# Keys, values and weight quantisation of the second layer moved into the expert stage of a two-layer gated cross-attention kernel

## The chip, the cores and the metric

The kernel runs on one core of a Trainium2 chip. The metric is the device time of one execution in microseconds (us), as the median of several runs. Engines: PE is TensorE, ACT is ScalarE, DVE is VectorE, POOL is GpSimd, SP is SyncE, which here only issues DMAs; SPq is SP's queue of DMA issues.

## What is computed

Two layers over 64 sequences of 128 tokens and 256 channels, in float32. Each layer adds a gated cross-attention and a gated feed-forward part to the residual:

```
x = x + tanh(g_xattn[0]) * attention0(layernorm(x), ctx)      # 16 heads of 16 channels, keys of one sequence: 128
x = x + tanh(g_ffn[0])   * experts(layernorm(x))              # router, 64 experts, top 8, at most 256 tokens each, + a shared one
x = x + tanh(g_xattn[1]) * attention1(layernorm(x), ctx, mask)
x = x + tanh(g_ffn[1])   * quantised_ffn(layernorm(x))        # int8-like activations and weights, 704 wide
```

Keys and values of both layers come from `ctx`, which no earlier step changes: `k = ctx @ wk.T + bk`, `v = ctx @ wv.T + bv`. A token's routing weight for an expert is `2.5 * sigmoid(logit) / (sum over its 8 chosen)`. The last part quantises its three weight matrices by row: `clip(round(w / scale)) * scale` with `scale = max|w| / 127`.

## The kernel before, in words

The work is in five phases, separated by `phase_end`, where all engines wait for each other.

1. Loads and constants.
2. First layer's attention, with router and shared expert. A loop over slots: in slot s each engine does its steps for several sequences at once, each at a fixed lag (`stage(lag)` is sequence s - lag). The residual lies in `res` (64 rows of 256 floats per partition). The part after the attention goes to memory: `store` puts residual plus shared expert into `accumulator`, `store_row` puts the normalised token with one float of routing share (`pay`, ROW = 257 floats) into `token_rows`. In the last slots, and after them, DVE quantises the weights of the last part (`weights_dve`), PE transposes them (`weights_pe`), ACT copies them (`weights_act`), SP stores them (`ffn_weights_out`). Before the phase ends, SP issues the second layer's weights (`attention_weights`) and the first experts' (`first_expert_weights`).
3. Experts (`experts_pe`, `_act`, `_dve`, `_pool`, `_sp`). One slot for each of 64 experts. DVE and PE work out which tokens an expert has (`slot_steps`, `tokens`), two slots ahead POOL gathers their rows from `token_rows` by two indirect DMAs (`gather`), PE transposes them (`rows_t`), multiplies by the two upper matrices (`up`) and, with 1-column products, by the router's column (the logits again), and then by the lower matrix (`down`). DVE multiplies by the routing weight (`outputs`), and POOL adds the rows to `accumulator` by two indirect DMAs (`add`). After the last expert PE and ACT make keys and values of sequences 0 to 2 (`first_keys_values_pe`, `_act`).
4. Second layer's attention: 64 slots and a few for the ends. For sequence b the steps are: SP loads the context `cx` and the two accumulators' rows `ax` (`load`, three slots ahead); DVE adds the two (`first_sum`, L852, two slots ahead) and takes statistics; ACT normalises; PE projects q, k and v (`project_qk` L434, `project_v` L449); ACT copies them out (`copy_qk` L621 and L624, `copy_v` L634); PE writes the mask and the scores into the four banks of `tiles` (L336, L352), DVE takes the maximum of all four (L810), PE writes mask and transposed scores into the same banks (L336, L369), ACT takes the exponent (L601), PE multiplies by the values (L399), transposes (L480), DVE divides (`head_norm`, L918), PE transposes back (`tokens_to_heads`, L490) and multiplies by the output matrix (L469).
5. The quantised part in two passes.

Each engine runs its own instructions strictly in the order written, and waits on counting semaphores. In phase 4 the order on DVE in a slot is: maximum, `first_sum`, `first_stats`, `head_sums`, `head_norm`, `token_maximum`, `residual`, and so on. On PE it is: mask and scores, the projections, mask and transposed scores, `heads_to_tokens`, `output`, `tokens_to_heads`, `transposes`, `maxima_t`, `values`. On SP it is only:

```
wait(sp, sm("v_done"), b - 3)
wait(sp, sm("qk_done"), b - 3)
load_context(sp, b, r)
...
wait(sp, sm("sum_done"), b - 1)
for n_ in range(2):
    sp.dma_start(ax[p][:, n_, :], acc[n_][bass.ds(b * P, P), :]).then_inc(sem(f"ax_in{p}"), 16)
```

`v_done` and `qk_done` count PE's projections. The first wait is for the projections of sequence b - 4.

Of the kernel before, what the change touches and what calls it, by code (L numbers as in the profile page):

```python
# [5 lines left out]
def flamingo_gated_two_layers(nc: bass.Bass, a, out: bass.AP):  # L6
# [25 lines left out]
    ROW = D + 1  # L32
    SHAREC = D
# [16 lines left out]
    KV_FIRST = 3  # L50
# [11 lines left out]
    hidden_away = nc.dram_tensor("hidden_away", [len(AWAY), P, IC * CT], f32).ap()  # L62
    ffn_int = nc.dram_tensor("ffn_int", [3, P, KC * IP], bf16).ap()

    ctx = ExitStack()
    with ctx:
# [86 lines left out]
        xr = ring("xr", 4, [P, HALVES, ROW])  # L153
        xrt = ring("xrt", 2, [P, KC, CAP])
        sg = ring("sg", 2, [P, CAP])
        he = ring("he", 2, [P, CAP])
        ye = ring("ye", 4, [P, HALVES, D])
        wcol = ring("wcol", 4, [P, HALVES])
        tid = ring("tid", 8, [P, HALVES], i32)
        ehs = ring("ehs", 2, [P, CAP])  # L160
        ren = ring("ren", 2, [P, HALVES])
# [52 lines left out]
        wraw = [qkp[:, 3 * n:3 * n + 3, :].rearrange("p a (c d) -> p (a c) d", d=D) for n in range(2)]  # L214
        wdraw = cxax[:, 0:6, :].rearrange("p a d -> p (a d)")[:, 0:KC * I].rearrange("p (k i) -> p k i", k=KC)
        wq_b = pt[1][:, 2:4, :].rearrange("p a d -> p (a d)").bitcast(bf16)[:, 0:KC * IP]
        ws = [w.rearrange("p a d -> p (a d)").bitcast(bf16)[:, 0:KC * IP] for w in (pt[0][:, 2:4, :], ovs[:, :, :], qkp[:, 0:2, :])]
# [78 lines left out]
        MADE_WEIGHTS = (8 if IREST else 6) * 2 + 11  # L296
# [26 lines left out]
        TILES_IN_0 = 8 * NB  # L323
# [3 lines left out]
        def attention_pe(pe, L):  # L327
            def sm(name):
                return f"{name}_{L}"

# [8 lines left out]
            def scores(m):  # L339
# [4 lines left out]
                wait(pe, sm("exp_done"), b - 1)  # L344
# [9 lines left out]
                last.then_inc(sem(sm("s_done")), 1)  # L354

            def scores_t(k):
# [4 lines left out]
                pe.wait_ge(sem(sm("max_done")), ahead(b, 2))  # L361
                if L == 1:
                    masks(1)
                pe.wait_ge(sem(sm("qm_done")), b + 1)
# [6 lines left out]
                last.then_inc(sem(sm("st_done")), 1)  # L371

            def maxima_t(m):

                if m is None:
                    return
                b, _ = m
                pe.wait_ge(sem(sm("max_done")), b + 1)
# [6 lines left out]
                nc.tensor.transpose(bk[:, 0:P], mt[:, :], ident[:, :]).then_inc(sem(sm("mt_done")), 1)  # L385

            def values(k):
# [5 lines left out]
                pe.wait_ge(sem(sm("exp_done")), b + 1)  # L393
                pe.wait_ge(sem(sm("v_out")), b + 1)
                wait(pe, sm("at_out"), b)
# [5 lines left out]
                last.then_inc(sem(sm("pv_done")), 1)  # L401

            def transposes(f):
# [8 lines left out]
                else:  # L412
                    wait(pe, sm("v_out"), b)
# [4 lines left out]
            def project_qk(f):  # L418
# [5 lines left out]
                pe.wait_ge(sem(f"tile_in{r}"), (2 - L) * (4 * (b - r) + 16) + L * TILES_IN_0)  # L424
# [5 lines left out]
                for j in range(KC):  # L430
                    for n, w in enumerate((w_q, w_k)[:1 if L == 1 and b < KV_FIRST else 2]):
# [4 lines left out]
                last.then_inc(sem(sm("qk_done")), 1)  # L436

            def project_v(f):
                if f is None or (L == 1 and f[0] < KV_FIRST):
                    return  # L440
                b, r = f
                pe.wait_ge(sem(f"tile_in{r}"), (2 - L) * (4 * (b - r) + 16) + L * TILES_IN_0)
                if L == 0:
                    wait(pe, sm("silu_done"), b - 4)
                    wait(pe, sm("qm_done"), b - 1)
                else:
                    pe.wait_ge(sem(sm("xt_out")), b + 1)
# [3 lines left out]
                last.then_inc(sem(sm("v_done")), 1)  # L451

            def output(k):
# [4 lines left out]
                pe.wait_ge(sem(sm("at_out")), b + 1)  # L458
                if L == 0:
                    wait(pe, sm("x2t_out"), b)  # L460
                else:
                    pe.wait_ge(sem(sm("qm_done")), ahead(b, 3))
# [10 lines left out]
            def heads_to_tokens(k):  # L473
# [4 lines left out]
                pe.wait_ge(sem(sm("ov_out")), b + 1)  # L478
                for g in range(NG):
                    last = nc.tensor.transpose(bank[7][:, g * P:(g + 1) * P], ov[r % 2][:, g, :], ident[:, :])  # L480
                last.then_inc(sem(sm("ot_done")), 1)

            def tokens_to_heads(k):
# [4 lines left out]
                pe.wait_ge(sem(sm("on_done")), b + 1)  # L488
                for c in range(KC):
                    last = nc.tensor.transpose(bank[7][:, c * P:(c + 1) * P], on[r % 2][:, c * P:(c + 1) * P], ident[:, :])  # L490
                last.then_inc(sem(sm("at_done")), 1)
# [11 lines left out]
            def moe_up(k):  # L503
# [7 lines left out]
                pe.wait_ge(sem(sm("qm_done")), ahead(b, 4))  # L511
# [46 lines left out]
            def body(stage):  # L558
# [17 lines left out]
                else:  # L576
                    project_qk(f)
                    project_v(f)
# [11 lines left out]
        def attention_act(act, L):  # L590
            def sm(name):
                return f"{name}_{L}"

            def exponent(k):
# [4 lines left out]
                act.wait_ge(sem(sm("st_done")), b + 1)  # L599
                wait(act, sm("pv_done"), b - 1)  # L600
                nc.scalar.activation(pt[r % 2][:, :, :], tiles[:, :, :], ACT.Exp).then_inc(sem(sm("exp_done")), 1)  # L601

            def copy_xt(f):
# [4 lines left out]
                wait(act, sm("qk_done"), b - 1)  # L608
# [3 lines left out]
            def copy_qk(f):  # L612
# [4 lines left out]
                act.wait_ge(sem(sm("qk_done")), b + 1)  # L617
                wait(act, sm("st_done"), b - 3)
                wait(act, sm("qm_done"), b - 1)
                for j in range(KC):  # L620
                    last = nc.scalar.activation(qt[p][:, j, :], bank[5][:, j * P:(j + 1) * P], ACT.Identity, bias=qb[:, j:j + 1])  # L621
                    if L == 0 or b >= KV_FIRST:
                        for e in range(2):
                            last = nc.scalar.activation(kp[r][:, e, j, :], bank[5][:, (KC + j) * P:(KC + j + 1) * P],  # L624
                                                        ACT.Identity, bias=kb[:, e, j:j + 1], scale=keep[:, e:e + 1])
                    last.then_inc(sem(sm("qk_out")), 1)

            def copy_v(f):
                if f is None or (L == 1 and f[0] < KV_FIRST):
                    return  # L630
                b, r = f
                act.wait_ge(sem(sm("v_done")), b + 1)
# [1452 lines left out]
```

## Time and profile before

| | |
|---|---|
| median of 3 runs | 2064.66 us (2063.12 to 2065.77) |
| profiled execution | 2069.3 us, of which the span is 2067.5 us |
| busy share of the span | PE 89%, DVE 68%, ACT 54%, POOL 27% |
| mean granted TensorE clock | 0.945 |
| phase 3, experts | 809.1 to 1246.4 us |
| phase 4, second attention, steady part | 1281 to 1837 us |
| chain that ended last | PE 66%, DVE 14%, issue 8%, POOL 5%, DMA 4%, ACT 2% |

Times in rows are microseconds from the start of the span unless marked ns. A timeline row is start, duration, engine, line, operation, output and inputs with their shapes and count, and in brackets the idle time of the engine before it with what ended it. A busy share over the whole span averages phases with different limits, so each phase is read alone.

### The profile page before, as it was taken

How to read it: one execution, taken by the hardware profiler on the slowest of the kernel's cores; microseconds unless marked ns; L12 is line 12 of the kernel's file. 1: busy time of each engine (PE TensorE's matmuls, PEld its weight loads, DVE VectorE, ACT ScalarE, POOL GpSimd, SP SyncE). 2: the span in 40 equal slices, each digit the busy share in tenths (PEclk: the TensorE clock that was granted, in tenths of full speed). 3: DMA queues.
4: the chain of work that ended last, by engine and by line, in shares of the span. 5: the costliest groups of instructions: out<-in, count | busy, mean ns of one | idle time of the engine just before them, and what ended most of it. 6: DMA issues, size and time to landing. Idle time of an engine off the chain costs nothing.

```text
span 2067.5 us, 55165 instructions
## 1 busy us (share of the span) xinstructions
PE 1832.9 (89%) x20966; PEld 1463.2 (71%) x20976; DVE 1402.3 (68%) x4715; ACT 1119.8 (54%) x2347; POOL 562.2 (27%) x551
## 2 busy tenths in 40 slices
PE   6999999999999994888778876999999999978855
PEld 4888888888888873666666664777777777753334
DVE  4778878787878776444444435666666666658988
ACT  3666666666666651111111124666666666658875
POOL 1000000000000001788888871111111111111147
PEclk9999999999999996888888888999999999999989
DMA  3122222222222215666666652111111111102355
GB/s 96 45 60 61 61 64 60 71 61 64 61 63 61 58 43 182 139 140 141 142 141 143 133 98 64 48 41 48 45 43 48 41 48 41 40 25 111 134 214 193
DMA packets 158646, 174.30 MB, mean 84 GB/s; under 512 B 22512, under 2 KB 142704, under 8 KB 156208
## 3 DMA queue, kind: packets, MB, share of 16 engines
q1 hardware_dynamic: 133568, 136.34, 21.9%
q0 software_dynamic: 24816, 34.42, 9.9%
q8 instruction: 170, 2.79, 0.6%
q14 instruction: 92, 0.75, 0.1%
HBM read 104.72 MB, written 65.98 MB: 83 GB/s over the span
## 4 chain that ended last, share of the span: by engine, by line
PE 66%; DVE 14%; issue 8%; POOL 5%; DMA 4%; ACT 2%; POOLq 0%; SPq 0%; DVEq 0%; ACTq 0%
PE bank L434 12%; PE tiles L369 7%; PE tiles L352 7%; PE bank L399 6%; PE bank L517 6%; PE bank L449 5%; PE bank L480 4%; PE bank L469 3%; PE bank L540 3%; PE tiles L1252 3%; DVE hmax L1660 2%; POOL accumulator L1457 2%; PE tiles L336 2%; POOL xr L1442 2%; DMA xr<-token_rows,tid 2%
## 5 line engine op out<-in xcount | busy, mean ns | idle before, releaser
L1920 POOL TENSOR_TENSOR rstd<-var,minus_half 128x2 f32<-128x2 f32 x138 | 96.1, 696 | 1142.9 <-DVE var L887 1142.7
L810 DVE TENSOR_REDUCE mt<-tiles 128x16 f32<-128x2048 f32 x128 | 293.5, 2293 | 113.6 <-PE tiles L352 113.6
L601 ACT ACTIVATE pt<-tiles 128x2048 f32<-128x2048 f32 x128 | 240.8, 1881 | 13.1 <-PE tiles L369 8.5
L1457 POOL DMA_INDIRECT accumulator<-ye,tid x128 | 205.0, 1601 | 42.8 <-issue 31.7
L624 ACT ACTIVATE qkp<-bank,kb,keep 128x128 f32<-128x128 f32 x500 | 205.2, 475 | 0.0
L1405 DVE TENSOR_SCALAR ye<-bank,wcol 128x256 f32<-128x256 f32 x128 | 56.0, 479 | 216.3 <-PE bank L1270 175.1
L434 PE MATMUL bank<-xt,w_q 128*128 128x128 f32 x1024 | 165.1, 285 | 0.9 <-ACT xt L609 0.9
L621 ACT ACTIVATE qkp<-bank,qb 128x128 f32<-128x128 f32 x256 | 96.0, 376 | 123.9 <-PE bank L434 123.7
L1442 POOL DMA_INDIRECT xr<-token_rows,tid x128 | 137.3, 1072 | 81.1 <-DVE within L1370 44.5
L434 PE MATMUL bank<-cxax,w_k 128*128 128x128 f32 x1000 | 154.3, 277 | 0.0
L434 PEld LDWEIGHTS bank<-xt,w_q 128*128 128x128 f32 x1024 | 136.8, 195 | 22.6 <-issue 20.9
L369 PE MATMUL tiles<-qm,qkp 32*128 32x128 f32 x4096 | 150.2, 283 | 1.4 <-DVE mt L810 1.4
L352 PE MATMUL tiles<-qkp 32*128 32x256 f32 x2048 | 148.1, 402 | 3.2 <-ACT qkp L624 3.2
L1321 ACT COPY xrt<-tiles 128x512 f32<-128x512 f32 x64 | 37.5, 586 | 206.6 <-PE tiles L1234 173.2
L369 PEld LDWEIGHTS tiles<-qm,qkp 32*128 32x128 f32 x4096 | 125.8, 186 | 27.2 <-issue 24.3
L399 PE MATMUL bank<-pt,vx 128*32 128x128 f32 x4096 | 138.4, 276 | 2.3 <-ACT pt L601 1.5
L434 PEld LDWEIGHTS bank<-cxax,w_k 128*128 128x128 f32 x1000 | 133.5, 194 | 0.0
L469 PE MATMUL bank<-w_o,at 128*128 128x256 f32 x512 | 131.8, 380 | 0.5 <-ACT at L676 0.5
L667 ACT COPY ovs<-bank 128x512 f32<-128x512 f32 x128 | 75.1, 587 | 102.2 <-PE bank L399 102.2
L449 PE MATMUL bank<-w_v,cxax 128*128 128x256 f32 x500 | 130.2, 383 | 0.0
L1234 PE MATMUL tiles<-ident,xr 128*128 128x128 f32 x256 | 53.0, 342 | 78.9 <-DMA xr<-token_rows,tid 78.9
L352 PEld LDWEIGHTS tiles<-qkp 32*128 32x128 f32 x2048 | 92.7, 185 | 34.9 <-issue 26.9
(255 smaller groups left out, 4079.3 us busy)
## 6 DMA issues: line engine op xcount, KB each, us to landing
cxax<-in_ctx SPq DMA_DIRECT2D x128, 128.0 KB, 2.6
cxax<-accumulator SPq DMA_DIRECT2D x128, 128.0 KB, 2.2
hidden_away<-h_ring SPq DMA_DIRECT2D x8, 1536.0 KB, 5.1
pt<-in_expert_up SPq DMA_DIRECT2D x36, 256.0 KB, 4.6
token_rows<-pay SPq DMA_DIRECT2D x64, 128.5 KB, 2.7
res<-in_x SPq DMA_DIRECT2D x64, 128.0 KB, 2.7
accumulator<-xa SPq DMA_DIRECT2D x64, 128.0 KB, 1.7
accumulator<-zt SPq DMA_DIRECT2D x64, 128.0 KB, 1.8
```

Source lines behind the costliest of these rows:

```text
L352: last = nc.tensor.matmul(both, qt[r % 2][rows, j, :], kp[r][rows, :, j, :], start=(L == 0), stop=True, skip_group_check=(L == 1))
L369: last = nc.tensor.matmul(tiles[:, i, n * P:(n + 1) * P], kp[r][rows, e, j, :], qm[rows, e, j, :], start=(L == 0), stop=True, skip_group_c ...
L399: last = nc.tensor.matmul(bank[7][32 * h:32 * h + 32, g * P:(g + 1) * P], vx[r][:, GH * g + h, :], pt[p][:, i, n * P:(n + 1) * P], start=T ...
L434: last = nc.tensor.matmul(o_, w[:, c, j * P:(j + 1) * P], (cx[r] if n else xt[p])[:, c, :], start=(c == 0), stop=(c == KC - 1))
L449: last = nc.tensor.matmul(bank[4][:, 0:D], cx[r][:, c, :], w_v[:, c, :], start=(c == 0), stop=(c == KC - 1))
L469: last = nc.tensor.matmul(bank[6][:, 0:D], at[r % 2][:, c, :], w_o[:, c, :], start=(L == 1 and c == 0), stop=(c == KC - 1))
L517: last = nc.tensor.matmul(bank[4][:, n * FS + j * P:n * FS + (j + 1) * P], w[:, c, j * P:(j + 1) * P], x2t[p][:, c, :], start=(c == 0), st ...
L601: nc.scalar.activation(pt[r % 2][:, :, :], tiles[:, :, :], ACT.Exp).then_inc(sem(sm("exp_done")), 1)
L624: last = nc.scalar.activation(kp[r][:, e, j, :], bank[5][:, (KC + j) * P:(KC + j + 1) * P], ACT.Identity, bias=kb[:, e, j:j + 1], scale=ke ...
L810: nc.vector.tensor_reduce(mt[:, :].rearrange("p (i n c) -> p i n c", i=RT, n=2 * KC)[:, :, :, 0], tiles[:, :, :].rearrange("p i (n k) -> p ...
L1442: nc.gpsimd.indirect_dma_start(out=xr[r][:, h, :], out_offset=None, in_=rows[:, :], in_offset=bass.IndirectOffsetOnAxis(ap=tid[n % 8][:, h ...
L1457: nc.gpsimd.indirect_dma_start(out=acc[p][:, :], out_offset=bass.IndirectOffsetOnAxis(ap=tid[b % 8][:, h:h + 1], axis=0), in_=ye[r][:, h, ...
```

## The change

- A row of `token_rows` takes the token's 64 routing weights (`pay`, ROW = 320 floats). The router products, their tanh (`route_tanh`) and `wcol` in the experts' phase go; `outputs` multiplies by a column of the gathered row. The gathered rows have 5 buffers, not 4.
- In each expert's slot PE makes keys or values of two sequences (`keys_or_values`: 4 products of 256 columns, even slots keys, odd slots values), ACT copies the bank out (`copy_pair`), SP stores it to `keys_values` (`keep_pair`, 256 KB) and loads the context of a later pair. The rows 8 to 55 of `res`, free in that phase, are the room.
- In phase 4 PE projects q alone. SP loads a sequence's keys and values (2 DMAs into `kvt`, two buffers) where it loaded the context, and ACT copies them from there. `first_keys_values_pe` and `_act` go.
- The quantisation of the weights leaves the end of phase 2: DVE takes one step of it in a slot of the experts, PE, ACT and SP in the slots of `WEIGHTS_AT` and `WEIGHTS_OUT_AT`. Its loads are issued when `xa_done_0` reaches 56.
- Semaphores of both attention phases count on over both layers (`first + b`), which changes no order.

```diff
-    ROW = D + 1
-    SHAREC = D
+    ROW = D + E
+    GATEC = D
+    ROWS_IN = 5
...
+        cxp = [room(44 + 2 * k, 2).rearrange("p (c e t) -> p c e t", c=KC, e=2) for k in range(4)]
+        kvs = [room(52 + 2 * k, 2) for k in range(2)]
+        ROOM_FROM, ROOM_TO = 8, 56
+        kvt = [cxax[:, 2 * k:2 * k + 2, :].rearrange("p a d -> p (a d)") for k in range(2)]
...
-                for n, w in enumerate((w_q, w_k)[:1 if L == 1 and b < KV_FIRST else 2]):
+                for n, w in enumerate((w_q, w_k)[:2 - L]):
...
                 else:
                     project_qk(f)
-                    project_v(f)
                     scores_t(k)
...
+                if L == 1:
+                    act.wait_ge(sem(f"kv_in{p}"), 16 * (b - p) + 32)
...
+                    k = bank[5][:, (KC + j) * P:(KC + j + 1) * P] if L == 0 else kvt[p][:, j * P:(j + 1) * P]
+                    for e in range(2):
+                        last = nc.scalar.activation(kp[r][:, e, j, :], k, ACT.Identity, bias=kb[:, e, j:j + 1], scale=keep[:, e:e + 1])
...
-                st.mark(V.tensor_tensor(pay[r][:, SHAREC:SHAREC + 1], wsum[:, 0:1], tg_route[:, 0:1], ALU.mult))
+                st.mark(V.tensor_scalar(pay[r][:, GATEC:GATEC + E], wun[:, :], wsum[:, 0:1], tg_route[:, 0:1], ALU.mult, ALU.mult))
...
-                if L == 0 or b >= KV_FIRST:
-                    wait(sp, sm("v_done"), b - 3)
-                    wait(sp, sm("qk_done"), b - 3)
+                if L == 0:
+                    wait(sp, "v_done", first + b - 3)
+                    wait(sp, "qk_done", first + b - 3)
                     load_context(sp, b, r)
...
                 else:
+                    wait(sp, sm("qk_out"), 2 * (b - 1))
+                    wait(sp, sm("v_out"), b - 1)
+                    sp.dma_start(kvt[p][:, 0:D].rearrange("p (c t) -> p c t", c=KC),
+                                 keys_values[b - p].rearrange("p (c e t) -> p c e t", c=KC, e=2)[:, :, p, :]).then_inc(sem(f"kv_in{p}"), 16)
+                    sp.dma_start(kvt[p][:, D:2 * D], keys_values[b - p + 1][:, p * D:(p + 1) * D]).then_inc(sem(f"kv_in{p}"), 16)
                     wait(sp, sm("sum_done"), b - 1)
                     for n_ in range(2):
                         sp.dma_start(ax[p][:, n_, :], acc[n_][bass.ds(b * P, P), :]).then_inc(sem(f"ax_in{p}"), 16)
...
+            def keys_or_values(e):
+                if e is None:
+                    return
+                n, _ = e
+                j = n // 2
...
+                pe.wait_ge(sem(f"pair_in{j % 4}"), 8 * (j - j % 4) + 32)
+                wait(pe, "kv_out", n)
+                for k in range(2):
+                    for c in range(KC):
...
+                        last = nc.tensor.matmul(bank[5][:, k * D:(k + 1) * D], weights_, moving, start=(c == 0), stop=(c == KC - 1))
+                last.then_inc(sem("kv_done"), 1)
...
-                for h in range(HALVES):
-                    for c in range(KC):
-                        last = nc.tensor.matmul(bank[7][:, h:h + 1], xrt[p][:, c, h * P:(h + 1) * P], w_gate[:, c, expert_of(b):expert_of(b) + 1],
-                                                start=(c == 0), stop=(c == KC - 1))
-                last.then_inc(sem("e_logit_done"), 1)
...
             def body(stage):
                 slot_steps(stage(-MAP_AHEAD))
                 rows_t(stage(0))
+                keys_or_values(stage(0))
                 up(stage(1))
                 down(stage(2))
...
-        def ffn_weights_out(sp):
-            for n in range(3):
-                sp.wait_ge(sem("w_t_out"), n + 1)
-                sp.dma_start(ffn_int[n], ws[n]).then_inc(sem("ffn_int_out"), 16)
...
+        WEIGHTS_AT = {8: 0, 9: 0, 13: 1, 14: 1, 20: 2, 21: 2, 23: 3}
+        WEIGHTS_OUT_AT = {11: 0, 16: 1, 23: 2}
...
-            attention_dve(dve, 0, ffn_weights)
-            for _ in ffn_weights:
-                pass
+            attention_dve(dve, 0)
```

In phase 4, SP's issues and the waits ahead of them (`cxax` is the tile that holds `cx`, `ax` and, in the change, `kvt`). Before, one sequence is three rows:

```order
L1090 DMA cxax<-in_ctx 128x2x128 [waits qk_done_1,v_done_1]
L1112 DMA cxax<-accumulator 128x256 [waits sum_done_1]
L1112 DMA cxax<-accumulator 128x256
L1090 DMA cxax<-in_ctx 128x2x128 [waits qk_done_1,v_done_1]
L1112 DMA cxax<-accumulator 128x256 [waits sum_done_1]
L1112 DMA cxax<-accumulator 128x256
```

In the changed kernel it is four:

```order
L1122 DMA cxax<-keys_values 128x2x128 [waits v_out_1,qk_out_1]
L1124 DMA cxax<-keys_values 128x256
L1127 DMA cxax<-accumulator 128x256 [waits sum_done_1]
L1127 DMA cxax<-accumulator 128x256
L1122 DMA cxax<-keys_values 128x2x128 [waits v_out_1,qk_out_1]
L1124 DMA cxax<-keys_values 128x256
L1127 DMA cxax<-accumulator 128x256 [waits sum_done_1]
L1127 DMA cxax<-accumulator 128x256
```

The accumulators' rows, which stood behind a wait for PE's projections of sequence b - 4, now stand behind a wait for ACT's copies of sequence b - 2 (`v_out_1`, `qk_out_1`).

On DVE, one slot of phase 4 in the changed kernel (`res<-cxax` is `first_sum` of sequence s + 2, `on` is `head_norm` of sequence s - 3); this order is that of before:

```order
L825 TENSOR_REDUCE mt<-tiles 128x16 [waits mt_done,s_done]
L867 TENSOR_TENSOR res<-cxax 128x256 [waits ax_in0]
L877 BN_STATS st<-res 128x6 [waits sum_done_1]
L924 RECIPROCAL rden<-bank 128x16 [waits ot_done]
L933 TENSOR_TENSOR on<-bank,rden 128x256 [waits at_done,rden_done]
```

Nothing moved here; `head_norm` and all that follows it stand behind the wait for `ax_in`.

## Rows read from the trace of the kernel before

**Rows 1.** Stretches: length, busy PE, PEld, DVE, ACT, POOL, granted clock, DMA share, GB/s.

```profile
809.10:1246.40 437.30, 344.57 (x1705) 281.83 (x1705) 191.65 (x873) 78.36 (x207) 342.24 (x256) 0.83 0.65 132
...
1281.00:1837.00 556.00, 546.57 (x8694) 412.29 (x8692) 372.05 (x834) 377.49 (x777) 84.08 (x118) 1.00 0.15 44
```

**Rows 2.** Timeline of PE in one slot of the second attention.

```profile
1547.87 0.43 PE L336 MATMUL tiles<-mask_bias,identb 32*32 32x512 bf16 x16
...
1549.31 0.71 PE L434 MATMUL bank<-xt,w_q 128*128 128x128 f32 x4
...
1551.20 1.03 PE L449 MATMUL bank<-w_v,cxax 128*128 128x256 f32 x4
1552.15 0.43 PE L336 MATMUL tiles<-mask_bias,identb 32*32 32x512 bf16 x16
...
1555.09 0.44 PE L490 MATMUL bank<-ident,on 128*128 128x128 f32 x2
...
1557.21 0.43 PE L336 MATMUL tiles<-mask_bias,identb 32*32 32x512 bf16 x16
```

**Rows 3.** Timeline of DVE, ACT and SP's queue in the same slot.

```profile
1549.45 2.29 DVE L810 TENSOR_REDUCE mt<-tiles 128x16 f32<-128x2048 f32 x1 [1.04 <-PE tiles L352]
...
1551.40 0.37 ACT L621 ACTIVATE qkp<-bank,qb 128x128 f32<-128x128 f32 x1 [1.82 <-PE bank L434]
1551.65 0.41 DVE L852 TENSOR_TENSOR res<-cxax 128x256 f32<-128x256 f32 x1
...
1552.26 0.38 SPq L1090 DMA_DIRECT2D cxax<-in_ctx  x1
...
1552.68 0.94 SPq L1112 DMA_DIRECT2D cxax<-accumulator  x2
1553.29 0.40 ACT L634 COPY vx<-bank 128x256 f32<-128x256 f32 x1
...
1554.32 0.26 DVE L909 RECIPROCAL rden<-bank 128x16 f32<-128x16 f32 x1 [1.79 <-PE bank L480]
1554.61 0.42 DVE L918 TENSOR_TENSOR on<-bank,rden 128x256 f32<-128x256 f32 x1
```

**Rows 4.** DMA issues: output<-input, count, size, median us from issue to landing.

```profile
cxax<-in_ctx SPq DMA_DIRECT2D x128, 128.0 KB, 2.6
cxax<-accumulator SPq DMA_DIRECT2D x128, 128.0 KB, 2.2
```

**Rows 5.** Timeline of DVE: first and last of the 64 maxima of the second attention.

```profile
1258.27 2.29 DVE L810 TENSOR_REDUCE mt<-tiles 128x16 f32<-128x2048 f32 x1 [1.86 <-PE tiles L352]
...
1836.98 2.29 DVE L810 TENSOR_REDUCE mt<-tiles 128x16 f32<-128x2048 f32 x1 [1.12 <-PE tiles L352]
```

**Rows 6.** Experts: PE's timeline around a wait, and the stretch behind it.

```profile
1109.84 0.66 PE L1234 MATMUL tiles<-ident,xr 128*128 128x128 f32 x4 [2.62 <-DMA xr<-token_rows,tid]
...
1113.14 1.71 PE L1258 MATMUL bank<-w_gate,xrt 128*128 128x1 f32 x8
...
1121.27 0.95 PE L1258 MATMUL bank<-w_gate,xrt 128*128 128x1 f32 x8
...
1110.90:1121.10 10.20, 10.20 (x33) 8.04 (x32) 2.87 (x13) 1.36 (x4) 8.06 (x8) 0.50 0.64 119
```

**Rows 7.** Groups of instructions: POOL's two indirect DMAs of the experts.

```profile
L1457 POOL DMA_INDIRECT accumulator<-ye,tid x128 | 205.0, 1601 | 42.8 <-issue 31.7
...
L1442 POOL DMA_INDIRECT xr<-token_rows,tid x128 | 137.3, 1072 | 81.1 <-DVE within L1370 44.5
```

**Rows 8.** End of phase 2: SP's last expert weights, quantisation steps, PE's next phase.

```profile
802.14 0.43 SPq L1181 DMA_DIRECT2D xt<-in_L_ffn_w  x1
...
L761 DVE TENSOR_REDUCE s_gu<-qkp 128x6 f32<-128x1536 f32 x2 | 3.5, 1748 | 0.2 <-DVE pt L775 0.2
...
L771 DVE TENSOR_SCALAR qkp<-qkp 128x1536 f32<-128x1536 f32 x2 | 1.9, 959 | 0.1
...
809.11 0.22 PE L1209 MATMUL bank<-table,halves_tri 128*128 128x32 bf16 x1 [1.17 <-SPq L257]
```

More of the change, by code:

```diff
@@ L343, in scores @@
                 b, r = m
-                wait(pe, sm("exp_done"), b - 1)
+                wait(pe, "exp_done", first + b - 1)
                 if L == 1:
@@ L435, in project_qk @@
                                                     start=(c == 0), stop=(c == KC - 1))
-                last.then_inc(sem(sm("qk_done")), 1)
+                last.then_inc(sem("qk_done"), 1)
             def project_v(f):
-                if f is None or (L == 1 and f[0] < KV_FIRST):
+                if f is None:
                     return
                 b, r = f
[L442 to L447, printed above, removed]
+                pe.wait_ge(sem(f"tile_in{r}"), 8 * (b - r) + 32)
+                wait(pe, sm("silu_done"), b - 4)
+                wait(pe, "qm_done", first + b - 1)
                 for c in range(KC):
@@ L794, in weights_dve @@
-            st.then(V.tensor_copy(at[0][:, :, :], s_d[:, :].unsqueeze(2).broadcast_to([P, KC, P])))
+            st.mark(V.reciprocal(sig[:, :], sig[:, :]))
+            st.mark(V.tensor_copy(at[0][:, :, :], s_d[:, :].unsqueeze(2).broadcast_to([P, KC, P])))
+            yield
+            for _ in range(5):
+                yield
             dve.wait_ge(sem("sd_t"), 1)
-            st.then(V.tensor_copy(sd_row[:, :], bank[1][:, 0:D]))
+            st.mark(V.tensor_copy(sd_row[:, :], bank[1][:, 0:D]))
@@ L1045, in body @@
                     routing(1)
-                    if v is not None and v[0] == NB - 1:
-                        next(ahead_of_time)
                     routing(1)
@@ L1082, in body @@
                     gate_scales()
-                if L == 0 and v is not None:
-                    for _ in range({NB - 3: 1, NB - 2: 1, NB - 1: 3}.get(v[0], 0)):
-                        next(ahead_of_time)
             attention_slots(body, FIRST[L])
@@ L1329, in gate_tanh, with copy_pair @@
                 nc.scalar.activation(sg[r % 2][:, :], bank[2 + r % 2][:, 0:CAP], ACT.Tanh, scale=0.5).then_inc(sem("e_sg_done"), 1)
[L1331 removed]
+            def copy_pair(e):
                 if e is None:
                     return
[L1334 to L1337 removed]
+                n, r = e
+                p = r % 2
+                act.wait_ge(sem("kv_done"), n + 1)
+                wait(act, f"kv_kept{p}", 8 * (n - p))
+                nc.scalar.copy(kvs[p], bank[5][:, :]).then_inc(sem("kv_out"), 1)
             def body(stage):
                 copy_t(stage(0))
+                copy_pair(stage(0))
                 gate_tanh(stage(1))
[L1342 removed]
+                if stage(0) is not None and stage(0)[0] in WEIGHTS_AT:
+                    next(weights, None)
+            weights = weights_act(act)
             expert_slots(body)
@@ L1425, in body @@
                 hidden(stage(1))
+                if stage(0) is not None and stage(0)[0] > 2 and stage(0)[0] != E // 4 and stage(0)[0] != E // 4 + 4:
+                    next(weights, None)
                 next_layer(stage(0))
+            weights = weights_dve(dve)
             begin()
```

314 lines of the change are left out of this document (152 added, 162 removed).

## The prediction

> **What bounds the kernel now.** I read the stretches first, because the phases have different limits. In the steady part of the second attention PE is busy 546.6 of 556 us at a granted clock of 1.00, that is 2.4 GHz, DVE 372, ACT 377, and DMA at a share of 0.15 [rows 1]. PE is the bound there. A slot lasts 9.3 us (mask of the scores at 1547.87, again at 1557.21) [rows 2]. The experts' stretch is another matter: PE 344.6 of 437.3 us at a clock of 0.83, DMA at 0.65. Its bound is POOL. Per expert it issues two gathers and two additions: (137.3 + 205.0) / 64 = 5.35 us, and about 0.3 us of issue ahead of each of the four (31.7 us over the additions' 104 or so), together 6.55 us, times 64 = 419 of the 437 us [rows 1, 7].
>
> Then I read one slot of the second attention engine by engine, to see what PE's neighbours do if PE is relieved, and for each load what it waits for [rows 2, 3]. That second question decides this case.
>
> **PE in the second attention.** The change takes k and v out of the slot. From the first q product to v are 1551.20 - 1549.31 = 1.9 us for two q and two k groups, so k is 0.95 us; v is 1.03 us [rows 2]. 64 slots less 3, times 2 us, would be 120 us. It isn't to be had. DVE's maximum over all four banks runs from 1549.45 to 1551.74, and the mask for the transposed scores overwrites those banks, so PE can write it at 1551.85 at the earliest; before it does so at 1552.15 [rows 2, 3]. The rest of the slot on PE is as before. Even if nothing else went wrong a slot would get 0.3 us shorter (9.0), and 63 of them 19 us.
>
> **The wait that comes in.** SP's list is strictly in order. Before, the accumulators' rows of sequence s + 2 could be fetched long ahead: SP waited only for projections of sequence s - 2. Now the two loads of keys and values stand ahead of them, behind the wait that ACT has copied keys and values of sequence s out of the same buffer, `v_out_1`. ACT does that in slot s. But DVE's `first_sum` in slot s is the one of sequence s + 2, and it needs those very rows. Behind it in DVE's list stand `head_norm`, for which PE's `tokens_to_heads` waits, and with it the transposes, maxima, values and the whole next slot; the next q, and so ACT's next copy, come after that. So a ring closes once a slot:
>
> - PE, slot start to q ready: ACT's first copy starts at 1551.40 before, 0.95 us earlier without k: 1550.45 - 1547.87 = 2.6 us [rows 2, 3].
> - ACT, six copies of q and k, one of v: 1551.40 to 1553.69 = 2.3 us. The source of four is now an SBUF tile, not a bank; I take the same time [rows 3].
> - SP, four DMAs at 0.47 us each (0.94 for two): the last one starts 1.4 us after the wait falls, and lands 2.2 us later; with 0.1 us for the semaphore 3.7 us. If it lands like the context's, with smaller pieces, it is 2.6 us and the term 4.1 [rows 3, 4].
> - DVE, `first_sum` 0.41, statistics about the same, then from the reciprocal (1554.32) to PE's transposes (1555.09) 0.77: 1.6 us [rows 2, 3].
> - PE, from there to the next slot's start: 1557.21 - 1555.09 = 2.1 us [rows 2].
>
> The sum is 12.3 us a slot with PE at 2.4 GHz. Beside this ring PE has the middle of the slot, 1552.15 to 1555.09 = 2.9 us, ready by 3.9 + 2.9 = 6.8 us after the slot's start; `tokens_to_heads` can run at 2.6 + 2.3 + 3.7 + 1.6 = 10.2 us. PE waits 3.4 us in one piece in each slot, and some 1.3 us for the maximum.
>
> **The clock.** In the experts' stretch, behind a wait of 2.62 us for gathered rows, the granted clock was 0.50 (1.2 GHz) for 10.2 us, and the same 8 products took 1.71 us in place of 0.95, 1.8 times [rows 6]. A clock of 0.83 on average means a third of that stretch at 1.2 GHz, with PE idle 21% [rows 1]. In the new slot PE is idle (3.4 + 1.3) / 12.3 = 38%, most of it in one wait longer than that one, and the part of PE that lies in the ring (2.6 + 2.1 = 4.7 us) comes right behind it. I set 60% of it at 1.2 GHz: 4.7 x 0.8 x 0.6 = 2.3, so 14.6 us a slot. The bounds are none (12.3) and all (4.7 x 0.8 = 3.8, so 16.1).
>
> The 64 maxima stand 1836.98 - 1258.27 = 578.7 us apart from first to last [rows 5]. The ring holds in the 61 or so slots in which a load is still to come; two at the end take 9.0. 61 x 14.6 + 18 = 909, **+330 us** (bounds +190 and +421). The exit of the phase is the same. The block for sequences 0 to 2 that goes lay beside POOL's last additions and is worth nothing.
>
> **End of phase 2.** SP's last expert weight is issued at 802.57, PE's next phase starts at 809.11; between lies only the quantisation [rows 8]. With some 0.4 us for the handshake 6 us go. DVE's reduction of 1.75 us and small steps among its last routing steps also held up the last token rows, so I take **-8 us** (bounds -5 and -9).
>
> **Experts.** POOL's instructions are the same in number; a gathered row is 1280 bytes, not 1028, which I cost at nothing, the addition of 1024-byte rows and the gather being told apart by their kind and not by size in [rows 7]. So this phase can win at most the 10 us or so in which POOL isn't busy. What is added per slot: PE 4 products of 256 columns, twice L449's 1.03, less 0.95 for the router's: +1.1 us on 344.6 / 64 = 5.4, which is still about POOL's 6.55, and denser work should lift the clock [rows 1, 2, 6]; ACT 0.6 us on 1.2; DVE some 18 us in all, in steps of at most 1.75 on 3 us a slot [rows 1, 8]; DMA 256 KB out and 128 KB in per slot and 252 bytes more per gathered row, 29 MB on 132 GB/s x 437 us = 58 MB. At the same efficiency the share would rise from 0.65 to 0.97, with larger pieces to some 0.9 [rows 1]. Gathers then land later, and PE already waited for them in [rows 6]. The cover is POOL's two-slot lead. I take **+12 us**, bounds -5 and +60.
>
> A page speaks against this part. The rows show the two kinds of steps, 1.75 us for 1536 floats and 0.96 for the same number, so the second kind runs in a fast mode [rows 8]; no row shows it beside a gather. The Trainium skill, SBUF — State Buffer, section "SBUF: two separate sides", says that while DVE runs such a two-port instruction POOL can't write its DMA descriptors. By that rule the six such steps, at no more than 0.96 us each, would hold up the phase's bound by up to 5.8 us (an estimate); the sum would be 5.8 higher, well inside the range.
>
> **Sum.** 2069.3 + 330 - 8 + 12 = 2403 for the profiled execution; it stands 4.6 above the median of the three runs (2064.66), so **2399 us**.
>
> **Rivals.**
>
> 1. The ring, but PE keeps 2.4 GHz. For it: a wait of 2.62 us was followed by the fall once in the rows I show, and the experts' stretch, with its many waits, still has two thirds of its time at 2.4 GHz [rows 1, 6]. Against it: here the wait is longer and comes in every slot. 12.3 us a slot, +190: 2259. Chance 0.17.
> 2. The ring, and PE stays at 1.2 GHz throughout. Against it: at 1.2 GHz the middle of the slot grows too, the long wait shrinks, and PE looks busy. 16.1 a slot, +421: 2490. Chance 0.13.
> 3. The ring, and the experts' phase turns DMA-bound. For it: 0.9 to 0.97. A slot of 7.7 in place of 6.8 there, +58 in place of +12: 2445. Chance 0.1.
> 4. The other side: the accumulators' rows land in time, since `first_sum` could be taken by DVE without a wait. Then only the maximum bounds the slot: -19 - 8 + 12, so 2050, faster. It decides at one point: the last of the four loads must be issued 2.2 us before the maximum ends, that is at 1549.5 in the slot of rows 3, while ACT's copies for which SP waits only begin at 1550.45. The order of the waits speaks plainly against it; what is left is that I misread a count. Chance 0.05. That the change doesn't relieve PE at all is part of this case: k and v are gone from its list.
>
> My own case has 0.55, with its own range of 2330 to 2450. A measurement of this kernel can tell about 0.2% (4 us) from no change. Faster 0.04, within 0.2% 0.01, slower 0.95. The range of 8 in 10 reaches from under rival 1 (2259 less 14 for a gain in the experts) to over rival 2 (2490): 2245 to 2500.
>
> **What would show it.** The maxima of DVE 14.6 us apart (12.3 to 16.1); L867, `first_sum`, with an idle time of some 5 us or more ahead of it in each slot, released by the DMA of the accumulators; PE idle over 3 us ahead of `tokens_to_heads`; a granted clock of about 0.7 in the phase; PE's idle ahead of the second mask released by the maximum. Phase 2 ends near 801; the experts last 430 to 450 us. I am wrong if `first_sum` doesn't wait, or if the accumulators' rows are issued before ACT's copy of v.

## The result, and the profile after

The changed kernel takes 2382.23 us in the median (2380.34 to 2384.68, 4 runs), the kernel before 2065.22 beside it; the ratio is 1.152 (95% interval 1.150 to 1.154). Forecast were 2399 us. The profiled execution has a span of 2381.3 us and a mean clock of 0.912.

By stretch, the experts and the steady second attention of the changed kernel (columns as in [rows 1]):

```profile
799.00:1241.20 442.20, 354.10 (x1707) 287.46 (x1707) 207.71 (x836) 104.22 (x198) 345.79 (x256) 0.93 0.83 198
1294.80:2117.90 823.10, 520.33 (x7582) 368.34 (x7583) 355.03 (x798) 376.62 (x741) 80.66 (x114) 0.85 0.13 38
```

PE was busy 98% of the second attention before and is now busy 63% of it, at a clock of 0.85 in place of 1.00 [rows 1]. The first and the last three of DVE's maxima:

```profile
1261.03 2.29 DVE L825 TENSOR_REDUCE mt<-tiles 128x16 f32<-128x2048 f32 x1
...
2132.92 2.29 DVE L825 TENSOR_REDUCE mt<-tiles 128x16 f32<-128x2048 f32 x1 [3.28 <-PE tiles L361]
2141.84 2.29 DVE L825 TENSOR_REDUCE mt<-tiles 128x16 f32<-128x2048 f32 x1 [1.11 <-PE tiles L361]
2150.75 2.29 DVE L825 TENSOR_REDUCE mt<-tiles 128x16 f32<-128x2048 f32 x1 [1.12 <-PE tiles L361]
```

From first to last they take 889.7 us, before 578.7 [rows 5]. A steady slot lasts 14.4 us. The two at the end, for which nothing is left to load, last 8.9. And these are the groups of instructions of the changed kernel that wait (columns: busy, mean ns, idle time before and its releaser):

```profile
L867 DVE TENSOR_TENSOR res<-cxax 128x256 f32<-128x256 f32 x64 | 27.2, 425 | 359.8 <-DMA cxax<-accumulator 359.8
L497 PE MATMUL bank<-ident,on 128*128 128x128 f32 x256 | 66.2, 348 | 235.6 <-DVE on L933 235.6
```

Before, `first_sum` waited for its rows once, 14.9 us at the phase's start. Now it waits 360 us in all, some 5.6 us in each slot, and PE's `tokens_to_heads` waits for `head_norm` behind it.

The whole difference of the two spans, 313.8 us, by place:

| | before | after | difference | forecast |
|---|---|---|---|---|
| start of the experts' phase | 809.1 | 799.0 | -10.1 | -8 |
| experts' phase | 437.3 | 442.2 | +4.9 | +12 |
| its end to the first maximum | 11.9 | 19.8 | +8.0 | not named |
| first to last maximum | 578.7 | 889.7 | +311.0 | +330 |
| from there to the end | 230.5 | 230.5 | 0 | 0 |

### The profile page after: what moved, and what is told of

Same layout as the page of the kernel before. It is cut to its first block, busy times and chain, and to the rows that moved or that the text cites. A ratio compares the mean times of both kernels' runs of the same rounds, so it can differ in the third digit from the quotient of the medians.

```text
span 2381.3 us, 53833 instructions
## 1 busy us (share of the span) xinstructions
PE 1840.3 (77%) x20198; PEld 1441.2 (61%) x20208; DVE 1409.2 (59%) x4649; ACT 1163.5 (49%) x2347; POOL 565.8 (24%) x551
## 4 chain that ended last, share of the span: by engine, by line
PE 55%; DVE 14%; DMA 10%; ACT 7%; issue 6%; SPq 5%; POOL 3%; POOLq 0%; ACTq 0%; DVEq 0%
PE bank L444 8%; PE bank L408 7%; PE tiles L361 6%; DMA cxax<-accumulator 6%; PE bank L524 5%; ACT qkp L633 4%; DMA xr<-token_rows,tid 4%; PE tiles L378 3%; PE bank L1268 3%; PE bank L476 2%; PE bank L456 2%; PE bank L547 2%; PE bank L497 2%; PE tiles L1300 2%; DVE hmax L1690 2%
## 5 line engine op out<-in xcount | busy, mean ns | idle before, releaser
L497 PE MATMUL bank<-ident,on 128*128 128x128 f32 x256 | 66.2, 348 | 235.6 <-DVE on L933 235.6
L867 DVE TENSOR_TENSOR res<-cxax 128x256 f32<-128x256 f32 x64 | 27.2, 425 | 359.8 <-DMA cxax<-accumulator 359.8
L688 ACT COPY at<-bank 128x256 f32<-128x256 f32 x128 | 47.6, 372 | 320.0 <-PE bank L497 320.0
L497 PEld LDWEIGHTS bank<-ident,on 128*128 128x128 f32 x256 | 29.2, 160 | 268.6 <-DVE on L933 260.9
L408 PE MATMUL bank<-pt,vx 128*32 128x128 f32 x4096 | 187.8, 342 | 1.7 <-ACT pt L608 1.2
L1422 DVE TENSOR_SCALAR ye<-bank,xr 128x256 f32<-128x256 f32 x128 | 56.0, 479 | 195.8 <-PE bank L1312 193.8
L361 PE MATMUL tiles<-qkp 32*128 32x256 f32 x2048 | 168.3, 447 | 3.4 <-ACT qkp L633 3.2
L1462 POOL DMA_INDIRECT xr<-token_rows,tid x128 | 140.4, 1097 | 71.4 <-DVE within L1390 35.4
L408 PEld LDWEIGHTS bank<-pt,vx 128*32 128x32 f32 x4096 | 137.9, 136 | 28.7 <-issue 15.8
L361 PEld LDWEIGHTS tiles<-qkp 32*128 32x128 f32 x2048 | 104.1, 210 | 46.2 <-issue 34.7
L345 PE MATMUL tiles<-mask_bias,identb 32*32 32x512 bf16 x2048 | 64.5, 453 | 84.9 <-DVE mt L825 84.9
```

The lines of the kernel that those rows point to most:

```text
L361: last = nc.tensor.matmul(both, qt[r % 2][rows, j, :], kp[r][rows, :, j, :], start=(L == 0), stop=True, skip_group_check=(L == 1))
L408: last = nc.tensor.matmul(bank[7][32 * h:32 * h + 32, g * P:(g + 1) * P], vx[r][:, GH * g + h, :], pt[p][:, i, n * P:(n + 1) * P], start=T ...
L1462: nc.gpsimd.indirect_dma_start(out=xr[n % ROWS_IN][:, h, :], out_offset=None, in_=rows[:, :], in_offset=bass.IndirectOffsetOnAxis(ap=tid[n ...
```

## The experiments

Each ran beside the kernel before on the same chip. "Slot" is the mean distance of DVE's maxima in the steady part of the second attention.

**e1: the accumulators' rows first.** In `load`, for the second layer:

```diff
+                    wait(sp, sm("sum_done"), b - 1)
+                    for n_ in range(2):
+                        sp.dma_start(ax[p][:, n_, :], acc[n_][bass.ds(b * P, P), :]).then_inc(sem(f"ax_in{p}"), 16)
                     wait(sp, sm("qk_out"), 2 * (b - 1))
                     wait(sp, sm("v_out"), b - 1)
                     sp.dma_start(kvt[p][:, 0:D].rearrange("p (c t) -> p c t", c=KC),
...
-                    wait(sp, sm("sum_done"), b - 1)
-                    for n_ in range(2):
-                        sp.dma_start(ax[p][:, n_, :], acc[n_][bass.ds(b * P, P), :]).then_inc(sem(f"ax_in{p}"), 16)
```

> The changed kernel with one edit: SP issues the accumulators' rows ahead of the wait for ACT's copies and of the two loads of keys and values. Theory (the ring through SP's list): first_sum no longer waits, the ring opens, and a slot of the second attention falls from 14.45 us (measured after the change) to about 9.0, bounded by the wait for DVE's maximum; 63 x 9.0 = 567 us from first to last maximum in place of 890, so about 2060 us. Rival (keys and values read back from memory come late, or the lower clock holds the slot by itself): the slot stays near 14.4 and the time near 2380.

Measured: 2047.69 us, 0.991 of before (0.989 to 0.993). Three lines in another order take 335 us off the changed kernel. The slot is 8.92 us, and from first to last maximum 557.7 us pass. The timelines of PE and DVE, a slot of e1:

```profile
1505.80 2.29 DVE L825 TENSOR_REDUCE mt<-tiles 128x16 f32<-128x2048 f32 x1 [1.05 <-PE tiles L361]
...
1508.01 0.41 DVE L867 TENSOR_TENSOR res<-cxax 128x256 f32<-128x256 f32 x1
1508.15 0.44 PE L345 MATMUL tiles<-mask_bias,identb 32*32 32x512 bf16 x16 [1.33 <-DVE mt L825]
```

`first_sum` starts as the maximum ends, without a wait. PE waits 1.33 us for the maximum, and the clock of the phase is 1.00. So the slot is near the 9.0 us that rival 4 named, with the wait that it named, and its time (2050) is what this kernel takes. The read-back of keys and values is in time. The rival of e1, that it isn't, has fallen.

**e3: the wait alone, in the kernel before.** Nothing else of the change is in it:

```diff
                 if L == 0 or b >= KV_FIRST:
-                    wait(sp, sm("v_done"), b - 3)
-                    wait(sp, sm("qk_done"), b - 3)
+                    if L == 0:
+                        wait(sp, sm("v_done"), b - 3)
+                        wait(sp, sm("qk_done"), b - 3)
+                    else:
+                        wait(sp, sm("qk_out"), 2 * (b - 1))
+                        wait(sp, sm("v_out"), b - 1)
                     load_context(sp, b, r)
```

> The kernel before with one edit: in the second attention SP's load of the context waits for ACT's copies of sequence b - 2 (as the change's loads of keys and values do) instead of PE's projections of b - 4; keys and values are still projected there. Theory: the wait by itself closes the ring. The slot is PE to v ready and ACT's copies 5.8 us, SP's three issues and the landing 3.3 to 4, DVE 1.6, PE 2.1 = 12.8 to 13.5 us, and 14 to 14.6 with part of PE's share at 1.2 GHz: about +300 us, 2350 to 2390. Rival (what costs is the traffic of keys and values or the room PE loses): no change, 2065 us.

Measured: 2357.66 us, 1.140 of before (1.138 to 1.142), a slot of 13.99 us. ACT's copy of v, SP's issues and `first_sum` in one slot:

```profile
1509.69 0.40 ACT L634 COPY vx<-bank 128x256 f32<-128x256 f32 x1
1510.16 0.38 SPq L1090 DMA_DIRECT2D cxax<-in_ctx  x1
1510.59 0.94 SPq L1116 DMA_DIRECT2D cxax<-accumulator  x2
1513.40 0.42 DVE L852 TENSOR_TENSOR res<-cxax 128x256 f32<-128x256 f32 x1 [5.25 <-DMA cxax<-accumulator]
```

SP issues the moment the copy has ended, and DVE waits 5.25 us. e1 shows that the ring is needed for the slowdown, e3 that it is enough.

**e4: the same wait, the accumulators' rows issued first behind it.**

```diff
                     wait(sp, sm("qk_out"), 2 * (b - 1))
                     wait(sp, sm("v_out"), b - 1)
+                    wait(sp, sm("sum_done"), b - 1)
+                    for n_ in range(2):
+                        sp.dma_start(ax[p][:, n_, :], acc[n_][bass.ds(b * P, P), :]).then_inc(sem(f"ax_in{p}"), 16)
                     sp.dma_start(kvt[p][:, 0:D].rearrange("p (c t) -> p c t", c=KC),
...
-                    wait(sp, sm("sum_done"), b - 1)
-                    for n_ in range(2):
-                        sp.dma_start(ax[p][:, n_, :], acc[n_][bass.ds(b * P, P), :]).then_inc(sem(f"ax_in{p}"), 16)
```

> The changed kernel; the wait for ACT's copies stays ahead of all four loads, but the accumulators' rows are issued before the keys and values. It measures what the two issues ahead of them cost in the ring. Theory: two issues of 0.6 us each less, and no packets ahead: 1.25 to 1.6 us off each of 62 slots of 14.45, so 2382 - 78 to 2382 - 99 = 2283 to 2304 us. Rival (the landing is late for other reasons, as by the clock or DVE): less than 20 us.

Measured: 2271.78 us, a slot of 12.61 us: 1.8 us less than the change's 14.4, or 110 us in all, a little more than expected. From the end of v's copy to `first_sum` it is now 1508.19 to 1511.13, 2.9 us, in this slot:

```profile
1507.80 0.39 ACT L647 COPY vx<-cxax 128x256 f32<-128x256 f32 x1
1508.25 1.26 SPq L1124 DMA_DIRECT2D cxax<-accumulator  x2
...
1511.13 0.42 DVE L867 TENSOR_TENSOR res<-cxax 128x256 f32<-128x256 f32 x1 [4.14 <-DMA cxax<-accumulator]
```

In the mean of the steady slots this stretch is 1.4 us shorter than the change's 4.2, as expected, and PE's two parts of the ring are together 0.5 us shorter. The shorter wait also leaves the clock higher (0.90 from first to last maximum, the change 0.84), so every 0.1 us between copy and landing is paid once a slot and somewhat more.

**e5: PE's long wait filled.** Ahead of `tokens_to_heads` in the second attention, with `FILL = 8`:

```diff
+                if L == 1:
+                    pe.wait_ge(sem(sm("qk_out")), 2 * ahead(b, 4))
+                    for _ in range(FILL):
+                        nc.tensor.matmul(bank[5][:, 256:512], w_k[:, 0, 0:P], w_k[:, 1, :], start=True, stop=True)
                 pe.wait_ge(sem("on_done"), first + b + 1)
```

> The changed kernel with 8 products of 256 columns into an unused part of a bank ahead of tokens_to_heads in the second attention, 3.5 us at 2.4 GHz, inside PE's wait of 3.8 to 4.1 us. Their results are not used. It measures what the clock costs in the ring. Theory: the clock of the phase goes from 0.85 to about 1.00, and the slot from 14.45 to the ring at 2.4 GHz, 12.3 plus the 0.7 by which the four DMAs were longer than predicted = 13.0: 62 x 1.4 = 87 us less, about 2295 us. Rival (the clock is no part of the ring): 2382 us or above.

Measured: 2324.45 us, 58 us less than the change, though PE has eight products a slot more to do. Its stretch, with the clock as the third number from the end:

```profile
1300.00:2050.00 750.00, 627.12 (x8509) 482.48 (x8509) 355.31 (x798) 373.43 (x743) 81.08 (x114) 1.00 0.14 42
```

PE around the filled wait, in the timeline (L499 is the filler, from the issue of its first product to the end of its last):

```profile
1603.95 3.62 PE L499 MATMUL bank<-w_k 128*128 128x256 f32 x16
...
1608.08 0.44 PE L502 MATMUL bank<-ident,on 128*128 128x128 f32 x2 [0.51 <-DVE on L938]
```

The clock is 1.00 and the slot 13.16 us, while `first_sum` still waits 366 us in all, and PE still waits for `head_norm` behind the filler in every steady slot (0.67 us in the mean). So the filler doesn't hold the ring up: the ring at 2.4 GHz is 13.2 us, and the clock costs the change's slot the rest, 1.2 to 1.3 us. Direction and mechanism are as expected. The gain was put at 87 us, half as much again as was measured: the ring is 13.2, not 13.0, and where no ring is left to close the filler only costs (the last two slots take 12.2 us, the change's 8.9, and the stretch behind the last maximum is 8 us longer).

**e2: e1, with two steps in the wait for the maximum.**

```diff
                     project_qk(f)
-                    scores_t(k)
                     heads_to_tokens(o)
                     output(w)
+                    scores_t(k)
                     tokens_to_heads(o)
```

> As e1_ax_first, and on PE heads_to_tokens and output of the second attention stand ahead of the mask and the transposed scores, in the place where PE waits for DVE's maximum. Theory: with the ring open PE waits some 1.3 us for the maximum in each slot, and the two steps moved (0.5 + 1.0 us) fill it: a slot of about 7.8 us, 63 x 7.8 = 491, about 1985 us. Then ACT with 7.15 us of work a slot is next. Rival (the wait isn't PE's bound, something else holds the slot at 9.0): about 2060 us as in e1.

Measured: 2052.43 us, 0.992 of before (0.990 to 0.994), a slot of 8.86 us. A miss by 67 us, and no better than e1. PE no longer waits for the maximum; the wait moved to another place of the slot, as the timeline of ACT and PE shows:

```profile
1507.32 1.88 ACT L608 ACTIVATE pt<-tiles 128x2048 f32<-128x2048 f32 x1 [0.45 <-PE tiles L378]
...
1509.09 0.37 ACT L688 COPY at<-bank 128x256 f32<-128x256 f32 x1
...
1509.60 1.08 PE L408 MATMUL bank<-pt,vx 128*32 128x128 f32 x32 [1.38 <-ACT at L688]
```

PE is through with its list early and waits for the exponent and the copy behind it ahead of `values`; only after `values` do the next scores come. The four banks of `tiles` are handed around: scores, maximum, transposed scores, exponent, and `values` of PE stands in this circle by its place in the list, though it doesn't touch the banks.

In e1 itself the exponent isn't yet in the chain. PE runs there from the maximum through its list to `values` with a wait of 0.15 us for DVE's `residual`, and `values` doesn't wait for ACT:

```profile
1511.90 0.30 PE L394 MATMUL bank<-ident,mt 128*128 128x128 f32 x1 [0.15 <-DVE res L850]
1512.13 1.08 PE L408 MATMUL bank<-pt,vx 128*32 128x128 f32 x32
```

So, by the order of these waits, two circles of nearly the same length stand beside each other: maximum and PE's list behind it (8.92 us, e1), and the banks' circle with the exponent (8.86 us, e2). `values` lies in both.

**e6: e1, with `values` out of both circles.** PE multiplies by the values behind the next slot's scores and q; ACT's copy of the result goes ahead of the next exponent:

```diff
                     project_qk(f)
+                    values(o)
                     scores_t(k)
...
                     maxima_t(m)
-                    values(k)
...
                     copy_v(f)
+                    copy_ov(o)
                     exponent(k)
...
-                    copy_ov(k)
```

> As e1_ax_first (the ring open), and in the second attention PE's values of a sequence stand behind the next slot's scores and q, in the place where PE waits for DVE's maximum; ACT's copy of them stands ahead of the next exponent. In e2_ax_first_filled the slot stayed at 8.86 us because PE waited 1.4 us for ACT ahead of values: the banks' chain of scores, maximum, transposed scores, exponent, at copy and values was the bound. Theory (that chain is the bound of the slot once the ring is open): with values out of it the chain is 0.4 + 1.1 + 2.3 + 0.4 + 1.2 + 1.9 + latencies = 7.6, PE's own list 7.5 and partly in its way, so a slot of about 8.0 us, 63 x 0.9 = 57 us less than e1, about 1990 us. Rival (DVE's or ACT's total, or the clock, bounds the slot near 8.9): about 2047 us as e1.

> The same kernel as e1_ax_first, on the chip of e6_values_in_gap, so that the two are compared on one chip: 2035 to 2050 us.

Measured on one chip: e6 1998.12 us, 0.967 of before (0.965 to 0.969), and e1 again 2047.22 (0.988 to 0.992). The slot is 8.13 us, 0.8 less than e1's, and 49 us in all. It is the fastest version found, 70 us under the kernel before on that chip and 384 under the change. Its stretch of the second attention:

```profile
1281.00:1740.00 459.00, 423.82 (x7540) 304.62 (x7536) 352.92 (x789) 366.36 (x738) 81.45 (x114) 1.00 0.22 67
```

PE is busy 92%, DVE 77%, ACT 80%. PE's wait for the maximum is down to 0.3 us. The slot stays above the 7.6 us of the banks' chain, because another circle is now the longest: the chain view of e6 runs through ACT's list (the normalisation, the copies of keys, v and `values`), PE's `heads_to_tokens`, DVE's steps up to the statistics and POOL back to ACT.

**e7 and e8: what covers the work added to the experts.** Both are e1 with one edit. e7 takes half of the key and value products away (`for c in range(1)` in `keys_or_values`), so half of the channels isn't summed; e8 stores each slot's 256 KB twice:

```diff
                 sp.dma_start(keys_values[n], kvs[p]).then_inc(sem(f"kv_kept{p}"), 16)
+                sp.dma_start(kv_copy[n], kvs[p]).then_inc(sem(f"kv_kept{p}"), 16)
```

> e1_ax_first with half of the key and value products of the experts' phase left out (one half of the channels of ctx isn't summed): 0.85 us of PE less in each of 64 slots at 2.4 GHz. Theory (POOL's 6.55 us per expert bounds the phase, PE's new work is covered): the phase keeps its 438 to 444 us, within 3 us, and the time stays near 2047. Rival (PE's new work costs the 5 us by which the phase grew, or more): the phase gets 5 us or more shorter.

> e1_ax_first with each slot's keys or values stored twice, the second time to a place that nobody reads: 256 KB more per expert, 16.8 MB in all, at a DMA share that was 0.83 in this phase after the change. Theory (POOL bounds, the share of 0.83 isn't yet a limit): the share rises towards 0.93 and the phase grows by 3 to 15 us, through later gathers. Rival (DMA already bounds the phase): it grows by 16.8 MB at the 213 GB/s moved there, 79 us. If transfers cost nothing here, 0.

Measured: 2044.5 and 2050.04 us. The experts' phase in e1 again, in e7 and in e8, one stretch of each kernel, in this order:

```profile
801.60:1244.50 442.90, 353.81 (x1707) 287.45 (x1707) 207.82 (x836) 104.22 (x198) 344.88 (x256) 0.93 0.83 198
```

```profile
798.60:1238.10 439.50, 315.26 (x1451) 250.72 (x1451) 207.74 (x836) 104.42 (x198) 345.71 (x256) 0.88 0.84 199
```

```profile
801.30:1244.10 442.80, 355.37 (x1707) 288.67 (x1707) 207.57 (x836) 104.44 (x198) 345.22 (x256) 0.92 0.91 235
```

39 us of PE less shorten the phase by 3.4 us (the times as a whole don't part the two kernels), and the clock falls from 0.93 to 0.88. Of the same experts' code, e1, e2, e4 and e6 take 441.4 to 443.5 us, so some 2 us of the 3.4 can be scatter; against the expectation's "within 3 us" it is just outside. 16.8 MB more leave the phase where it was, at a DMA share of 0.91. e8's expected 3 to 15 us didn't come; a phase with a DMA share of 0.83 still had room.

POOL's 345 us busy are the same in all. In the changed kernel it runs from 24 to 423 us after the phase's start without a pause of more than 0.4 us, with 0.3 us ahead of nearly every instruction, and the three kernels here have at most one longer pause there (1.4 us). So it is the bound, as the prediction read it. The pauses are at the two ends of the phase, the long one ahead of the first addition. Before:

```profile
831.16 1.63 POOL L1457 DMA_INDIRECT accumulator<-ye,tid  x1 [2.44 <-DVE ye L1405]
```

In the change:

```profile
823.05 1.63 POOL L1477 DMA_INDIRECT accumulator<-ye,tid  x1 [6.50 <-DVE ye L1422]
```

This is also where half of the products less gains its time: ahead of the first and of the last additions e7 pauses 5.2 and 0.7 us, e1 again 6.5 and 1.4.

## Why the prediction was right

- **The ring.** All five steps of it were read from the order of the waits and are there. `first_sum` idle 5.6 us a slot (said: 5 or more), PE idle ahead of `tokens_to_heads` 3.7 to 4.8 us, 4.0 in the mean (said: over 3), maxima 14.4 apart (said: 14.6). e1 and e3 show it from both sides.
- **The size of its terms.** That 14.6 lies so near 14.4 is in part luck: two errors stood against each other. The ring at 2.4 GHz was put at 12.3 us and is 13.2, and the clock was given 2.3 us and takes 1.3. Means over the steady slots, in us:

| step of the ring | said, at 2.4 GHz | e5, at 2.4 GHz | the change |
|---|---|---|---|
| PE, slot start to ACT's first copy | 2.6 | 2.7 | 3.2 |
| ACT, seven copies | 2.3 | 2.45 | 2.45 |
| end of the copies to `first_sum` | 3.7 | 4.4 | 4.2 |
| DVE, `first_sum` to PE's `tokens_to_heads` | 1.6 | 1.6 | 1.6 |
| PE, from there to the next slot's start | 2.1 | 2.1 | 3.1 |
| sum | 12.3 | 13.2 | 14.5 |

  ACT takes 2.45 us, since a pair of copies that reads `kvt` took 0.87 us where the bank gave 0.80 to 0.82. SP's loads of `keys_values` took 0.52 and mostly 0.60 us to issue, not 0.47, and the rows landed later, so that it is 3.9 to 4.8 us from the copy's end to `first_sum` in the change and not 3.7. The rows below are of the changed kernel.

```profile
1617.51 0.39 ACT L647 COPY vx<-cxax 128x256 f32<-128x256 f32 x1
1617.97 0.52 SPq L1122 DMA_DIRECT2D cxax<-keys_values  x1
...
1618.54 0.60 SPq L1124 DMA_DIRECT2D cxax<-keys_values  x1
...
1619.18 0.90 SPq L1127 DMA_DIRECT2D cxax<-accumulator  x2
1621.85 0.43 DVE L867 TENSOR_TENSOR res<-cxax 128x256 f32<-128x256 f32 x1 [5.26 <-DMA cxax<-accumulator]
```

- **The clock.** It was given 2.3 us a slot and takes 1.2 to 1.3. The share of PE's part of the ring at 1.2 GHz, 60%, was argued from a ratio of idle times and came out about right; its price was too high. Behind the long wait, from `tokens_to_heads` to the next slot's start, the granted clock was 0.54 in the mean of the steady slots, that is 1.2 GHz nearly throughout, and from there to ACT's first copy 0.80. That is some 4.1 of 6.2 us at 1.2 GHz. But the first of these pieces grew from 2.1 to 3.1 us by it, 1.5 times, and not 1.8 times as the eight products of [rows 6]. The two pieces together cost 1.5 us, of which the faster landing than in e5 gives 0.2 back; why the rows land faster isn't shown. A granted clock of about 0.7 in the phase was said, and it was 0.85. The prediction's own sum gives more than 0.7: 60% of 4.7 us, 1.8 times as long, are 5.1 of 14.6 us at half the clock, which is 0.83. In the slot above, PE and the clock between its transposes and ACT's first copy of q (in the two stretches the clock is the third number from the end):

```profile
1608.43 0.69 PE L497 MATMUL bank<-ident,on 128*128 128x128 f32 x2 [4.11 <-DVE on L933]
...
1611.56 0.65 PE L345 MATMUL tiles<-mask_bias,identb 32*32 32x512 bf16 x16
...
1614.16 1.25 PE L444 MATMUL bank<-xt,w_q 128*128 128x128 f32 x8
```

```profile
1608.43:1611.56 3.13, 3.12 (x37) 2.29 (x38) 2.46 (x9) 0.74 (x2) 0.70 (x1) 0.50 0.01 3
1611.56:1615.45 3.89, 3.86 (x44) 2.43 (x40) 1.15 (x1) 1.57 (x3) 0.72 (x1) 0.64 0.02 4
```

  1608.43 to 1611.56 is 3.1 us, 2.1 in [rows 2]. The products of q take 1.25 us, nearly the 1.16 that they take in e5 at 2.4 GHz.
- **PE's relief isn't to be had.** Right: with the ring open (e1) the slot is 8.92 us, 0.36 under the 9.3 of before, where the arithmetic of PE alone would have given 7.3. The prediction took the maximum as the bound. e2 and e6 make this more exact: the maximum is one step of a circle that PE's list closes, and the banks' circle with the exponent is as long. Filling the wait for the maximum with steps that lie in one of them alone gains nothing (e2); filling it with `values`, which lies in both, gains 0.8 us a slot (e6).
- **End of phase 2.** -10.1 where -8 was said. One and the same kernel, e1, starts the experts' phase at 794.8 us in one profile and at 801.6 in another, so a difference of 2 us says nothing.
- **Experts.** +4.9 where +12 was said. POOL's own account gives it: 3.5 us more busy (342.2 to 345.8) and some 2 us more of waits ahead of its first addition. DMA at 0.83 was feared too much. The clock rose from 0.83 to 0.93; that denser work lifts it fits e7, where it is 0.88 with fewer products.
- **Start of the second attention.** +8 us from the phase's start to the first maximum had no term. Before, SP fetched three pairs of accumulators' rows at once at 1246.4, since the first three sequences needed no context. In the change the first pair stands behind two other loads, and the third behind ACT's first copy of v; in e1 this start is again short.
- **The Trainium skill's rule.** SBUF — State Buffer, "SBUF: two separate sides", was weighed at up to 5.8 us for DVE's fast one-input steps. Beside the six of them the trace shows three of POOL's additions and gathers some 0.3 us longer than the others, and the rest as long as ever. The longer stretch came from the multiplication with two inputs in SBUF:

```profile
875.25 1.75 DVE L777 TENSOR_TENSOR res<-res,inv 128x1536 f32<-128x1536 f32 x1
875.31 2.62 POOL L1462 DMA_INDIRECT xr<-token_rows,tid  x1 [0.31 <-issue]
```

  A gather takes 1.07 us in the mean of [rows 7]. Here it took 2.62, as long as DVE's step and 0.9 more; beside the other two such multiplications a gather was 0.8 and 0.6 us longer, and it too ended 0.9 us behind DVE's step. All gathers together rose from 137.3 to 140.4 us, so the rule's price was 4 us at most of the phase's 4.9. No run took these steps away. By the same section, a DVE instruction with two SBUF inputs contends with a GpSimd instruction that reads SBUF, and the trace agrees, if the gather's reading of its indices counts as that.

## What to carry to other kernels

A DMA queue's list is a chain like an engine's: when a load gets a later wait, every load behind it in the list gets that wait too, and the question is which of them is needed first. Put the load that is needed earliest ahead of the wait that falls latest, and look for a ring: here a copy at the end of a slot released a load that the same slot's middle needed. When work is taken off a bound engine, look at the circle that its buffers make before counting the gain; a step that doesn't touch the buffers may stand in it by its place in the list alone, and moving it (e6) was worth 0.8 us a slot, more than the 0.36 us that came of taking 2 us of products away (e1).

## What the runs showed of the hardware that I had not expected

Filling a wait with products whose results nobody uses made the kernel faster, 2382 to 2324 us, by keeping the granted clock at 1.00. Doubling a store of 256 KB per expert at a DMA share of 0.83 cost nothing that can be measured. A gather of POOL that started beside a two-input DVE instruction over 1408 or 1536 floats took 0.6 to 1.5 us longer, in all three cases. In the change, behind a wait of PE of 4.0 us in the mean, the granted clock was 0.54 over the next 3.1 us (1.2 GHz for most of them), slot after slot, and 1.00 again from ACT's first copy on; in e5, with 0.67 us of wait left there, it was 0.99.
